# Channel products of a pair block as f16 high and low parts, with their sums moved into the choice of experts

## What is computed

```
z    = layernorm(layernorm(x))                       # 256 x 64 x 128
ab   = sigmoid(z @ gate_w + gate_b) * (z @ lin_w + lin_b) * z_mask      # 256 x 64 x 64
g    = sigmoid(z @ eg_w + eg_b)
block1[i,j,c] = sum_k protein_pair[i,k,c] * ab[k,j,c]     # k over 256
block2[i,j,c] = sum_k ab[i,k,c] * compound_pair[j,k,c]    # k over 64
x    = x + g * (layernorm(block1 + block2) @ as_w + as_b) * z_mask
t    = x + mixture of the two best of 8 experts of layernorm(x)
```

## Time and profile before

| | |
|---|---|
| median of three runs | 1164.69 us (1159.89 to 1182.2) |
| profiled execution | 1164.22 us |
| its span, first to last instruction | 1162.4 us |
| TensorE busy in the span | 965.9 us, 83% |
| VectorE / ScalarE / GpSimd busy | 56% / 48% / 50% |
| first stage | until about 178 us |
| products of h = 0, then its normalising stage | 189 to 257 us, 257 to 364 us |
| products of h = 1, then its normalising stage | 382 to 450 us, 450 to about 565 us |

### The profile page before, as it was taken

One profiled execution on the slowest core, in us unless ns is written; L12 is line 12 of the kernel. 1 busy time (PEld: TensorE's weight loads), 2 busy tenths in 40 slices (PEclk: granted clock), 3 DMA queues, 4 the chain that ended last, 5 costly groups with the idle time before them and its releaser, 6 DMA issues. The chain is left out here.

```text
span 1162.4 us, 26502 instructions
## 1 busy us (share of the span) xinstructions
PE 965.9 (83%) x7510; PEld 764.3 (66%) x7511; DVE 656.4 (56%) x2206; ACT 552.2 (48%) x1247; POOL 581.1 (50%) x622
## 2 busy tenths in 40 slices
PE   1999998987995996898382698898898689899995
PEld 1445557984765995475220587787788578888884
DVE  6446762007675202778642577777777466666673
ACT  1335652114442112443410576676677467677773
POOL 2335651004331543876887255564556356656564
PEclk9999997555565555656555799999999899999998
DMA  7436710005560102235342233333333243444441
GB/s 194 133 118 184 217 70 37 1 29 183 175 193 1 37 32 87 79 120 166 122 148 77 73 120 100 114 112 108 107 110 96 77 121 109 124 115 119 117 122 41
DMA packets 111182, 124.56 MB, mean 107 GB/s; under 512 B 22110, under 2 KB 74359, under 8 KB 111131
## 3 DMA queue, kind: packets, MB, share of 16 engines
q1 hardware_dynamic: 91036, 80.92, 24.8%
q0 software_dynamic: 15296, 34.64, 8.5%
q10 hardware_dynamic: 4800, 8.39, 1.9%
HBM read 77.21 MB, written 49.09 MB: 109 GB/s over the span
## 5 line engine op out<-in xcount | busy, mean ns | idle before, releaser
L998 DVE TENSOR_TENSOR AB<-AB 128x512 f16<-128x512 f32 x280 | 191.7, 685 | 55.2 <-ACT AB L662 54.2
L516 POOL DMA_INDIRECT row_dram<-B x140 | 143.0, 1021 | 123.2 <-DVE B L1004 85.2
L516 POOL DMA_INDIRECT out<-B x140 | 143.9, 1028 | 103.9 <-DVE B L1004 57.2
L659 ACT ACTIVATE AB<-ps 128x512 f16<-128x512 f32 x280 | 168.2, 601 | 42.2 <-PE ps L1171 41.3
L1188 PE MATMUL ps<-PPb,AB 128*128 x1120 | 187.4, 221 | 0.0
L1189 PE MATMUL ps<-PPb,AB 128*128 x1120 | 187.0, 221 | 0.0
L662 ACT ACTIVATE AB<-ps 128x512 f32<-128x512 f32 x280 | 169.1, 604 | 0.0
L1169 PE MATMUL ps<-B,PPb 128*128 128x256 f16 x560 | 155.5, 278 | 0.0
L1170 PE MATMUL ps<-B,PPb 128*128 128x256 f16 x560 | 155.5, 278 | 0.0
L1171 PE MATMUL ps<-B,PPb 128*128 128x256 f16 x560 | 155.4, 277 | 0.0
L1191 PE MATMUL ps<-PPb,AB 128*128 x1120 | 155.2, 220 | 0.0
(11 more groups left out here) (225 smaller groups left out, 1988.3 us busy)
## 6 DMA issues: line engine op xcount, KB each, us to landing
B<-row_dram SPq DMA_DIRECT2D x70, 264.0 KB
PPb<-in_L_conv_protein_pair SPq DMA_DIRECT2D x32, 512.0 KB, 4.8
B<-row_dram SPq DMA_DIRECT2D x70, 136.0 KB
rows<-in_x SPq DMA_DIRECT2D x32, 256.0 KB, 2.8
g_dram<-work ACTq DMA_DIRECT2D x32, 256.0 KB, 2.0
work<-g_dram SPq DMA_DIRECT2D x32, 256.0 KB, 2.8
ABT<-in_x SPq DMA_DIRECT2D x32, 256.0 KB, 3.0
row_dram<-work SPq DMA_DIRECT2D x9, 264.0 KB, 2.7
```

The lines of the kernel that those rows point to most:

```text
L516: pool.indirect_dma_start(out_rows if second else row2_dram, bass.IndirectOffsetOnAxis(ap=Rw[:, u, b, at:at + 1].bitcast(u32), axis=0), Rw ...
L659: act.activation(Hp[:, hs, 0, :], ps[HB[hs]][:, :], ACT.Gelu, scale=1.0 / SCALE)
L998: dve.tensor_tensor(Hp[:, hs, 1, :], Hf[:, q, :], Hp[:, hs, 0, :], ALU.subtract).then_inc(h_parts[q], 1)
```

## The change

Every f32 value of the channel products becomes two f16 values, a high part and what is left of it, the low part, scaled by 16 first.

- `ab` is masked in place, then VectorE copies the high part to AB16 and GpSimd subtracts for the low part (`ab_low`). It lies so that 64 high and 64 low columns are one moving block of 128.
- A `protein_pair` piece is loaded to a slot (four in the first stage, two in the normalising stage of h = 0). ScalarE makes its high part (`pp_high`), VectorE its low part (`pp_low`), each 1024 values a partition, read in the order q, i out of a slot laid out i, q. SyncE waits for `pp_split` before it uses a slot again. In the lists of the normalising stage `pp_high1` stands at lag 1 and `pp_low1` at lag 2, both for h = 0 only.
- The transposes are f16, 64 instead of 32 a half, and ScalarE copies 1024 f16 values a bank.
- A pair of channels takes two products of 256 columns and eight of 128 columns, all f16, in 16 banks a half instead of 8. A bank now holds, for each channel, the sums of the high and of the low columns; VectorE adds the two (`evict`, a reduction of 512 PSUM values to 256 of B) in place of ScalarE's copy.
- For h = 0 VectorE makes these sums in a row. For h = 1 they stand between the steps of the first half's choice, which is now issued at the head of h = 1; `ranks(0)` stands after the eighth bank on TensorE, and ScalarE's `weights(0)` after the copies of the transposes.
- The compound values are split by VectorE in four passes instead of copied in two; the epsilon of the norm is scaled along.

The diff, cut to its core:

```diff
@@ sync
-            def pp_piece(h, n):
+            def pp_piece(h, n, slot, done):
-                sp.dma_start(PPb[:, bass.ds(n * 8, 8), :], ppv[:, h, bass.ds(n * 8, 8), :]).then_inc(pp_loaded[h], 16)
+                sp.dma_start(slot, ppv[:, h, bass.ds(n * 8, 8), :]).then_inc(done, 16)
...
                 if u % 2:
-                    pp_piece(0, n // 2)
+                    if not isinstance(n, int) or n >= 8:
+                        sp.wait_ge(s.pp_split, n - 7)
+                    pp_piece(0, n // 2, PPs0[:, u // 2, :, :], pp_in0[u // 2])
...
                     if h == 0:
-                        pp_piece(1, n)
+                        sp.wait_ge(s.pp_split, n * 2 + 30 if not isinstance(n, int) or n >= 2 else 32)
+                        pp_piece(1, n, PPs1[:, u % 2, :, :], pp_in1[u % 2])
@@ gpsimd
+            def ab_low(q, v):
+                for g in range(2):
+                    n = q * 2 + g
+                    pool.wait_ge(s.ab_hi, n + 1)
...
+                    pool.tensor_tensor(view(1), sg[:, g, :, :].rearrange("p t (a d) -> p t a d", d=2), view(0), ALU.subtract).then_inc(s.abm_done, 1)
-            pipeline(pool, GROUPS // 2, 2, [(0, rs_x), (2, mask_g)])
+            pipeline(pool, GROUPS // 2, 2, [(0, rs_x), (2, mask_g), (2, ab_low)])
@@ scalar
+            def pp_high(slot, m):
+                return act.activation(PPh[:, 0, :, bass.ds(m * 8, 8)], slot.rearrange("p i q -> p q i"), ACT.Copy, scale=PSCALE)
...
-            pipeline(act, GROUPS, 8, [(0, norm_x), (1, zT_copy), (2, sig), (4, g_store)], depth=4)
+            pipeline(act, GROUPS, 8, [(0, norm_x), (1, zT_copy), (2, sig), (2, pp_high0), (4, g_store)], depth=4)
...
-                    act.activation(ABT[:, 4 * m:4 * m + 4, :].rearrange("p a i -> p (a i)"), ps[m % 2][:, :], ACT.Copy).then_inc(s.abT_copied, 1)
-                for m in range(8):
-                    act.wait_ge(s.blk_done, h * 8 + m + 1)
-                    act.activation(B[:, :, 8 * m:8 * m + 8].rearrange("p j c -> p c j"),
-                                   ps[2 + m % 4][:, :].rearrange("p (c j) -> p c j", c=8), ACT.Copy).then_inc(s.blk_copied, 1)
+                    act.activation(ABT16[:, 4 * m:4 * m + 4, :, :].rearrange("p a r i -> p (a r i)"), ps[m % 2][:, :].bitcast(f16), ACT.Copy).then_inc(s.abT_copied, 1)
+                if h:
+                    weights(0)
...
+                def pp_high1(n, u):
+                    if h == 0:
+                        act.wait_ge(pp_in1[u % 2], (n // 2) * 16 + 16)
+                        pp_high(PPs1[:, u % 2, :, :], n).then_inc(s.pp_hi, 1)
...
-                                      (6, await_logit), (4, x1T_copy), (6, logit_copy)],
+                                      (6, await_logit), (4, x1T_copy), (1, pp_high1), (6, logit_copy)],
@@ vector
+            def pp_low(slot, m):
+                return dve.scalar_tensor_tensor(PPh[:, 1, :, bass.ds(m * 8, 8)], slot.rearrange("p i q -> p q i"), PSCALE,
+                                                PPh[:, 0, :, bass.ds(m * 8, 8)], ALU.mult, ALU.subtract)
...
+            def evict(h, m):
+                dve.wait_ge(s.blk_done, BANKS * h + m + 1)
+                parts = ps[2 + m % 4][:, :].rearrange("p (c r j) -> p c j r", c=4, r=2)
+                dve.tensor_reduce(B[:, :, 4 * m:4 * m + 4].rearrange("p j c -> p c j"), parts, AX.X, ALU.add).then_inc(s.blk_copied, 1)
...
-                dve.wait_ge(s.blk_copied, 8 * h + 8)
+                if h == 0:
+                    dve.wait_ge(s.cp_done, 4)
+                    for m in range(BANKS):
+                        evict(0, m)
+                else:
+                    choose(0, {2: [0], 4: [1], 6: [2], 8: [3], 10: [4], 12: [5], 14: [6], 16: [7], 19: [8], 20: [9], 21: [10], 22: [11], 23: [12],
+                               24: [13], 25: [14, 15]})
+                dve.wait_ge(s.blk_copied, BANKS * (h + 1))
...
+                def pp_low1(n, u):
+                    if h == 0:
+                        dve.wait_ge(s.pp_hi, n + 17)
+                        pp_low(PPs1[:, u % 2, :, :], n).then_inc(s.pp_split, 2)
-                pipeline(dve, GH, 4, [(X1LAG, gate_b), ((0, X1LAG), statistics), ((1, X1LAG + 1), deviations)],
+                pipeline(dve, GH, 4, [(X1LAG, gate_b), ((0, X1LAG), statistics), ((1, X1LAG + 1), deviations), (2, pp_low1)],
@@ tensor
-                if h:
-                    ranks(0)
...
+                    if h and m == 8:
+                        ranks(0)
+                    for a in range(2):
+                        pr = 2 * m + a
+                        o = ps[2 + m % 4][:, a * 256:(a + 1) * 256]
+                        cps = CP16[:, 2 * pr:2 * pr + 2, :, :].rearrange("p c r j -> p (c r j)")
+                        pe.matmul(o, ABT16[:, pr, 0, :], cps, start=True, stop=False)
+                        pe.matmul(o, ABT16[:, pr, 1, :], cps, start=False, stop=False)
                         for d in range(2):
...
+                            for g in range(IC):
+                                for r in range(2):
+                                    i = pe.matmul(o, PPh[:, r, g * C + 2 * pr + d, :], AB16[:, g, pr, :, d, :],
+                                                  start=False, stop=(d == 1 and g == 1 and r == 1))
```

More of the change, by code:

```diff
@@ L32 @@
 SCALE = 16.0
+PSCALE = 16.0
+BANKS = C // 4
 ROW = D + 8
@@ L147, in build @@
         xr = rows[:, :, :].rearrange("p j r -> p (j r)")[:, 0:8 * TG * E].rearrange("p (s t e) -> p s t e", s=8, t=TG)
+        PPs0 = rows[:, :, :].rearrange("p j r -> p (j r)")[:, 4096:8192].rearrange("p (s i q) -> p s i q", s=4, i=8)
         work = sb("work", [P, 5632])
@@ L178, in build @@
         ident = sb("ident", [P, P])
+        ident16 = sb("ident16", [P, P], f16)
         K8 = sb("K8", [P, NE])
@@ L277, in build @@
         g_loaded = [sem(f"g_loaded{u}") for u in range(4)]
-        pp_loaded = [sem(f"pp_loaded{u}") for u in range(IC)]
+        pp_in0 = [sem(f"pp_in0_{u}") for u in range(4)]
+        pp_in1 = [sem(f"pp_in1_{u}") for u in range(2)]
         moved = [sem(f"moved{u}") for u in range(4)]
@@ L641, in _ @@
                     a.then_inc(s.am_done, 1)
-                weights(2 * h)
+                    weights(2)
             for e in range(NE):
@@ L763, in _, with choose @@
                 lo, hi = q * C, (q + 1) * C
-                dve.tensor_copy(CPz[lo:hi, q::2, :], CPraw[lo:hi, :, q::2].rearrange("k j c -> k c j")).then_inc(s.cp_done, 1)
-            def choose(b):
+                raw = CPraw[lo:hi, :, q::2].rearrange("k j c -> k c j")
+                dve.tensor_scalar(CP16[lo:hi, q::2, 0, :], raw, PSCALE, None, ALU.mult).then_inc(s.cp_done, 1)
+            for q in range(2):
+                lo, hi = q * C, (q + 1) * C
+                raw = CPraw[lo:hi, :, q::2].rearrange("k j c -> k c j")
+                dve.wait_ge(s.cp_done, q + 1)
+                dve.scalar_tensor_tensor(CP16[lo:hi, q::2, 1, :], raw, PSCALE, CP16[lo:hi, q::2, 0, :],
+                                         ALU.mult, ALU.subtract).then_inc(s.cp_done, 1)
+            def evict(h, m):
+                dve.wait_ge(s.blk_done, BANKS * h + m + 1)
+                parts = ps[2 + m % 4][:, :].rearrange("p (c r j) -> p c j r", c=4, r=2)
+                dve.tensor_reduce(B[:, :, 4 * m:4 * m + 4].rearrange("p j c -> p c j"), parts, AX.X, ALU.add).then_inc(s.blk_copied, 1)
+            def choose(b, between={}):
                 h, j0, j1 = BATCHES[b]
@@ L775, in tail @@
                     dve.wait_ge(s.tail, tails[0])
+                    for m in between.get(tails[0] - TAIL * b, ()):
+                        evict(1, m)
                 over = lambda a, shape: a.rearrange("p (t o) -> p t o", o=1).broadcast_to(shape)
@@ L1055, in _ @@
                     for a in range(4):
-                        c = 2 * (4 * m + a)
-                        i = pe.transpose(ps[m % 2][:, a * P:(a + 1) * P], AB[:, h, c:c + 2, :].rearrange("p c j -> p (c j)"), ident[:, :])
+                        for r in range(2):
+                            k = (2 * a + r) * P
+                            i = pe.transpose(ps[m % 2][:, :].bitcast(f16)[:, k:k + P],
+                                             AB16[:, h, 4 * m + a, r, :, :].rearrange("p d j -> p (d j)"), ident16[:, :])
                     i.then_inc(s.abT_psum, 1)
-                if h:
-                    ranks(0)
                 pe.wait_ge(s.abT_copied, h * 8 + 8)
-                pe.wait_ge(pp_loaded[h], 16 * 16)
-                pe.wait_ge(s.cp_done, 2)
-                PPv = PPb[:, :, :].rearrange("p i (k c) -> p k i c", c=C)
-                for m in range(8):
+                pe.wait_ge(s.pp_split, 32 * (h + 1))
+                pe.wait_ge(s.cp_done, 4)
+                for m in range(BANKS):
                     if m >= 4:
-                        pe.wait_ge(s.blk_copied, 8 * h + m - 3)
+                        pe.wait_ge(s.blk_copied, BANKS * h + m - 3)
                     elif h:
```

73 lines of the change are left out of this document (44 added, 29 removed).

## The result

The changed kernel takes 1237.91 us (median of 4 runs, 1229.04 to 1241.26), the kernel before 1169.93: ratio 1.06, 95% interval 1.0484 to 1.0715. It is slower, and 1237.91 lies in the forecast range; 1224 was forecast. The profiled execution took 1229.04 us, the least of the four, with a span of 1227.3, 64.9 us more than the span before.

The account below looks back on a forecast made before the run. Bounds: TensorE always busy in the first stage and products (mostly at its lower level there), 85% busy in normalising. From 1164.22 us, 24 + 6 - 45 + 77 - 2 = +60 gives 1224 us; range 1182 to 1266.

Parts of the forecast that it names:

- Products of the first half: First half's channel products, now f16: 24 us with the last sum instead of 69, -45, with -26 as the other end.
- The upper level: First half's products: TensorE at 2.4 GHz, 0.67 us a pair of channels, 21.4 us; 43 at the lower level.
- The 3 us at the lower level: Start of the first half's products: some 3 us at TensorE's lower level, making 23 us of 21.4.
- First stage: Stage before the products: added copies and low parts make VectorE the bound, +24 us (+16 at 1.2 us a copy).
- VectorE becomes the bound of the second part: First stage, part at the upper level: VectorE needs 9.8 us a pair of groups, more than TensorE's 7.6.
- the third rival: First stage: TensorE falls back once it waits for VectorE, 13.5 us a pair instead of 9.8; 1244 to 1264; 20%.
- they are short: First stage: the argument that TensorE's waits for VectorE are short, set against its falling back to the lower level.
- Between the stage and the products: Between first stage and products: two more VectorE passes and longer ScalarE bank copies, +6 us (4 to 9).
- Normalising stage: First half's normalising stage: VectorE and ScalarE take turns over the pieces, 185 us against 107, +77.
- The turn: Normalising stage: VectorE's 4.24 us, ScalarE's 2.81, two copies of 1.9 and handovers in sequence, 11.1 us.
- The second rival: Pieces in the first and normalising stages: strided copies cost 1.2 us instead of 1.9; +24, 1188 us; 17%.
- Second half: Second half: first power waits behind 28 row moves, 85 to 91 us after the choice begins; -2 (-4 to +2).

Follow-up runs that it names:

- run 7: Changed kernel without VectorE's and GpSimd's additions in the first stage (low parts, copy to f16; low values filled with zeros once): 1172.26 us, 1.0279.
- runs 5: Changed kernel with 24 spare f16 products on TensorE behind each group's projections from the first stage's ninth group on: 1221.51 us, 1.0686.
- run 1: Changed kernel with VectorE's low part of a piece one step later in the normalising stage (lag 3 for 2): 1171.53 us, 1.014.
- run 3: Changed kernel with both copies of a piece reading their 1024 values side by side instead of 512 bytes apart: 1201.16 us, 1.0448.
- run 4: Changed kernel with the first half's choice made in one go, ahead of the 16 sums of the second half's banks: 1217.23 us, 1.0605.
- run 6: Changed kernel with the low part one step later and the first half's choice in one go ahead of the sums: 1144.6 us, 1.0014.
- run 2: Changed kernel without the 16 low parts of the pieces in the first stage (zeros filled once by GpSimd): 1229.47 us, 1.0629.

## Why the prediction was right, and where it was off

The spans differ by 64.9 us, and this is where they lie, forecast first:

- Products of the first half: -45, measured -46.3 (68.5 to 22.2). The upper level was taken, and it held: TensorE is busy 21.44 us, as 32 x 0.67 had it. The 3 us at the lower level that the sum added stand in no row of the prediction and did not come in this execution; in run 7 the products began at granted 0.50 (166.3 to 170.0 us). By the Trainium skill (TensorE: Matmul & The Clock Gate, Part 1: The HAM clock gate) activity releases the throttle; the trace agrees here, at granted 1.00. No run here shows why the f32 products did not keep it. Windows of the kernel before show that they began near the upper level and lost it with TensorE busy throughout, so a wait is not the only thing that can bring a fall (columns as in the earlier trace rows):

```profile
188.90:194.40 5.50, 5.50 (x29) 5.50 (x29) 0.00 (x0) 0.00 (x0) 0.00 (x0) 0.94 0.01 3
194.40:257.00 62.60, 62.60 (x293) 62.60 (x293) 0.00 (x0) 7.22 (x7) 0.00 (x0) 0.50 0.00 1
```

- First stage: +24, measured +41.7 (last projection at 218.8 instead of 177.1). This is the step that was off. "VectorE becomes the bound of the second part" held for a few pairs: 10.1 to 10.7 us each, 9.8 forecast. But TensorE then waits, loses its level, and the pair costs 13.5 us again; VectorE, which was to be without waits, is busy 92.55 of 127.70 us. I had that as the third rival at 20%, with "they are short" against it; the waits were 1.3 to 3.1 us, and runs 5 and 7 show that without them the level stays. These 41.7 us hold for two executions; in the other three kernels with this first stage the first product came 2.6 to 12.1 us later.
- Between the stage and the products: +6, measured +7.2 (19.0 against 11.8).
- Normalising stage: +77, measured +70.3, the term that decided. The turn is 10.78 us against 11.1, VectorE's waits 4.4 us against "about 5", and run 1 takes the turn away. The copies were sized right: 1.92 and 1.93 us against 1.9; run 3 shows that the stride is the reason. By the Trainium skill (Advanced Engine Details and Errata, SBUF Cachelines) an access that moves to another 16-byte line each time pays a penalty; run 3 agrees, with 1.05 and 1.23 us side by side. Why the plain copy of 2048 values did not pay it stays open. The second rival, 1.2 us, falls with the measured 1.92.
- Second half: -2, measured -9.9. The mechanism is as forecast, the first power behind 28 row moves (run 4). The size was off since a sum took 0.69 us and not 1.0, so that the first row move came 42.4 us after the choice began and not 48 to 54.
- The rest: 0, measured +1.9.

So too little in the first stage (18 us) and too much in the normalising stage and the second half (15 us) nearly cancelled. That the total came so near is luck; that the kernel is slower, and by the turns in the main, is not. The profiled execution lies 5 us above the forecast, the median 14.

## What to carry over

Where a piece of work is handed from one engine's pipeline to another's, look at what each of them does between the hand-overs: if each waits behind a step that releases the other, they take turns, and one more step between making and using, where there is a slot for it, parts them. A faster stage gives nothing when work that used to lie under it, here 28 row moves, starts only at its end. And an engine that is filled up makes TensorE wait; the price of that was here not the wait but the clock: 13.5 us a pair instead of 10.

## What was not expected of the hardware

The time at which TensorE's level first rises is not fixed by the program. TensorE was busy without a wait from about 26 us on, and the pace changed at about 76 us in the changed kernel, 95 in run 1, 128 in run 4 and 157 in run 6, which all have the same first stage. In others it changed at 95 us (the kernel before), 115 (run 2), 128 (run 3) and 28.9 (run 7). In the kernel before a pair takes 13.5 us until then and 7.6 after it, so that each 13.5 us of delay cost it 5.9. The kernel before took 1135.85 to 1202.97 us in its 27 executions beside the runs; whether this delay is what parts them is not shown, since only one execution of it was traced. What sets that time none of these rows shows.

GpSimd can hold up VectorE for a whole operation. Timelines of the changed kernel, VectorE and GpSimd:

```profile
18.62 0.17 DVE L744 TENSOR_TENSOR mv<-stats 128x8 f32<-128x8 f32 x1
...
19.26 0.17 DVE L752 SCALAR_TENSOR_TENSOR mv<-mv 128x8 f32<-128x8 f32 x1
...
90.22 0.39 DVE L744 TENSOR_TENSOR mv<-stats 128x8 f32<-128x8 f32 x1
...
91.36 1.29 DVE L748 TENSOR_SCALAR mv<-mv 128x8 f32<-128x8 f32 x1
...
92.69 0.17 DVE L752 SCALAR_TENSOR_TENSOR mv<-mv 128x8 f32<-128x8 f32 x1
...
91.25 1.37 POOL L465 TENSOR_TENSOR AB<-work,AB 128x256 f32 x1
```

The operation L748 on 8 values, 0.17 us in the median, took 1.29 and ended with GpSimd's low part, at 92.65 and 92.62 us. In the kernel before the same operation never took over 0.174. In run 7 a VectorE operation that starts at 16.98 us took 3.38 us and ended with a fill that GpSimd had begun at 16.83. By the Trainium skill (SBUF — State Buffer, SBUF: two separate sides) some VectorE operations need a pair of ports that they share with GpSimd, and one of the two holds it for a whole instruction; these rows agree. So GpSimd's new low part also lengthens VectorE's pair, which was not in the sum. From the start of L744 to that of L752 2.47 us passed there instead of the 0.64 of the first pair, right ahead of TensorE's wait of 2.86 us and the first fall; most pairs of the changed kernel kept 0.65. How much of the first stage GpSimd cost was not measured by itself.
